# GNN layer with residual and norm on one core: fewer TensorE signals, and GpSimd's gathers no longer tied to the other engines' progress

## The chip, the cores and the metric

One NeuronCore of one Trainium2 chip. Five engines take part: TensorE (PE, with PEld its weight loads), VectorE (DVE), ScalarE (ACT), GpSimd (POOL), and SyncE (SP), which only issues transfers. They run their own streams of instructions and meet by semaphores: an instruction can add one to a semaphore when it is finished (a signal, `then_inc`), another engine waits until the semaphore has reached a value (`wait_ge`). The metric is the device time of one execution in microseconds, the median of several; less is better.

## What is computed

```python
proj = einsum('ni,rio->nro', x, relation_weight)          # x: 50000 x 64, 10 relations
att  = sum(proj[src, etype] * tanh(proj[dst, etype] + efeat), -1)   # 25000 edges
ex   = exp(att - segment_max(att, dst)[dst]);  a = ex / segment_sum(ex, dst)[dst]
h_nb = segment_sum(x[src] * a[:, None], dst)              # dst is sorted
gnn  = leaky_relu((x + h_nb) @ fc.T, 0.01) + leaky_relu((x * h_nb) @ fc2.T, 0.01)
out  = layernorm(x + gnn)
```

A row of x that is nobody's dst has h_nb = 0: its output needs only the dense product with fc. All is float32.

## The kernel before

**Two kinds of work.** The dense part takes the 50,000 rows of x as 49 tiles d of 1024 rows: transpose, product with fc, relu, residual, norm, store. The edge part takes the 25,000 edges as 196 columns of 128 edges, in 25 blocks s of 8 columns (the last has 4). Each dst row that has edges is overwritten at the end with its edge result.

**The steps.** One loop of steps s = -1 to 28 runs on TensorE, ScalarE and VectorE with the same index (PE lines 627 to 701, ACT 814 to 902, DVE 1143 to 1299). In step s stand the relation products of block s, the scores and running sums of block e = s-1, the two residual products of block f = s-2, the norms of l = s-3 and o = s-4, and up to three dense tiles. Dense tiles end in step 15. From LATE = 14 on, the products of a block f take another way (`late_y`, `late_linear`), in the PSUM room that the dense tiles leave. So steps up to 15 are the dense steps, those from 16 the late ones.

**Relation products.** TensorE makes ten "quads" a block (`quad`, L545): four products of 64x64 tiles each, accumulated into t_ps and h_ps. Nine of them read a masked copy of the block's transposed rows, which VectorE makes (`mask`, L989, 9 a block, ring xm of RM = 4 buffers); the fifth (PLAIN_AT = 4) reads an unmasked copy by ScalarE. Mask m may be written once the quad that read mask m-4 has signalled (L995). Quad 9 ends a block: then come ACT's tanh (L710), DVE's product (L1003), PE's scores (L532), the next block's transposes (`turn_in`, L520) and ACT's copy of them (`plain`, L716), and the next block's first mask.

**Signals of TensorE.** Every quad signals (quad_done), as do the edge additions (eadd_done), the transposes (tr_in: three dense tiles and two groups a step, all through one PSUM tile, tr_ps), the dense products (y_done), the scores (att_done), `turn_in` (xT_done) and each quarter of a block's residual products (y12_done). ACT copies out of PSUM what each of them tells of (dT L721, rd L726, uwT L785, l L790), and later PE instructions wait for those copies.

**GpSimd.** POOL issues all indirect transfers, one instruction for a column of 128 rows: 388 gathers of x rows (L450) into a ring xsd of RX = 13 blocks, then 196 scatters of results (L474) from a ring out_r of RW = 18 blocks. Gathering block s waits for the last sum of block s-13 (z2_done, L444). The scatters wait until all dense tiles are stored (L466), and each block's for its result (fmul_done, L470). Besides, POOL is tied to the others' progress: `pace` (L435) makes it wait before an indirect transfer until TensorE has signalled a given place of its stream. The places come from `pe_marks` (L252), which lists all TensorE signals with the count of PE instructions up to each; gather n asks for the mark at n x 14.6 - 250 instructions. `load_e` on SP (L357) waits for eadd_done of three blocks before.

Of the kernel before, what the change touches and what calls it, by code (L numbers as in the profile page):

```python
# [12 lines left out]
P = 128  # L13
# [11 lines left out]
RM = 4  # L25
# [6 lines left out]
PACE, LEAD, PACE_OUT = 14.6, 250, 13.64  # L32
# [8 lines left out]
def gnn_resnorm(nc, x, src, dst, eattr, etype, relw, resw, resw2, out):  # L41
# [17 lines left out]
    def groups(s):  # L59
        return cols(s) // QUAD  # L60
# [4 lines left out]
    Q_BEFORE = [2 * n for n in G_BEFORE]  # L65
# [18 lines left out]
    def quad_count(m):  # L84
        return m // RB * R + m % RB + (2 if m % RB >= PLAIN_AT else 1)

    LATE = (ND - 1) // 3 - 2
    ROW_BLOCKS = [8, 13, 19, 24]
# [20 lines left out]
    with ExitStack() as ctx:  # L109
# [105 lines left out]
        xT_done, masked, quad_done, eadd_done = sem("xT_done"), sem("masked"), sem("quad_done"), sem("eadd_done")  # L215
# [35 lines left out]

        def pe_marks():  # L252

            marks, work, ends = [], [0], {}

            def mark(done, value, instructions):
                work[0] += instructions
                marks.append((done, value, work[0]))

            for s in range(-1, LAST + 1):  # L260
                main, e, f, d = 0 <= s < NS, s - 1, s - 2, tiles(s)
                quarters = 2 * groups(f) if 0 <= f < NS else 0

                def turned(k):
                    if len(d) > k:
                        mark(tr_in, TR_DENSE[d[k]] + 1, 8)

                def multiplied(k):
                    if len(d) > k:
                        mark(y_done, d[k] + 1, 16)  # L270

                def quads(first, last):
                    if main:
                        for r in range(first, last):
                            mark(quad_done, s * R + r + 1, 16)

                def paired(q):
                    if quarters > q:
                        mark(y12_done, Q_BEFORE[f] + q + 1, 8)

                turned(0)
                if main:
                    mark(eadd_done, s + 1, 2 * cols(s))
                if 0 <= e < NS:
                    mark(att_done, e + 1, 2 * cols(e))
                multiplied(0)
                quads(0, 4)
                if quarters > 0:
                    mark(tr_in, TR_PAIR[f, 0] + 1, 8)
                quads(4, 5)  # L290
                if quarters > 2:
                    mark(tr_in, TR_PAIR[f, 1] + 1, 8)
                quads(5, 6)
                paired(0)
                turned(1)
                quads(6, 7)
                paired(1)
                multiplied(1)
                quads(7, 8)
                paired(2)  # L300
                turned(2)
                quads(8, 9)
                paired(3)
                multiplied(2)
                quads(9, 10)
                if 0 <= s + 1 < NS:
                    mark(xT_done, s + 2, 2 * cols(s + 1))
                ends[s] = work[0]
            return marks, ends
# [4 lines left out]
        def _(sp):  # L314
# [42 lines left out]
            def load_e(s):  # L357
                if not 0 <= s < NS:
                    return
                wait(sp, eadd_done, s - RE + 1)  # L360
                c0, n = s * COLS, cols(s)
                n2 = min(n, LASTC - c0)
                done = e_in[s % RE]
                sp.dma_start(ea[0:A0, s % RE, 0:n, :], edge_rows[0:A0, c0:c0 + n, :]).then_inc(done, DMA)
                sp.dma_start(ea[A0:P - 1, s % RE, 0:n, :], edge_rows[A0:P - 1, c0:c0 + n, :]).then_inc(done, DMA)
                if n2 > 0:
                    sp.dma_start(ea[P - 1:P, s % RE, 0:n2, :], edge_last[:, c0:c0 + n2, :]).then_inc(done, DMA)
# [54 lines left out]
        def _(pool):  # L422
# [6 lines left out]
            G_MOVES = [0]  # L429
            for s in range(NS):  # L430
                G_MOVES.append(G_MOVES[-1] + len(columns(s)))

            (marks, ends), at = pe_marks(), [-1]

            def pace(n, scattered_blocks):  # L435
                step_end = ends[min(NS - 1, RW + 4 + scattered_blocks)]
                asked = min(n, G_MOVES[NS]) * PACE + max(n - G_MOVES[NS], 0) * PACE_OUT - LEAD
                need = [k for k, (_, _, work) in enumerate(marks) if work <= min(asked, step_end)]
                if need and need[-1] > at[0]:
                    at[0] = need[-1]  # L440
                    pool.wait_ge(marks[at[0]][0], marks[at[0]][1])

            def gather(s):
                wait(pool, z2_done, s - RX + 1)  # L444
                for k, (j, side) in enumerate(columns(s)):
                    pace(G_MOVES[s] + k, 0)
                    if s == 0 and (j, side) == (0, 1):
                        pool.wait_ge(dst_in, 4 * DMA)
                    c = s * COLS + j
                    pool.indirect_dma_start(  # L450
                        xsd[:, s % RX, j, side, :], None, x[:, :],
                        bass.IndirectOffsetOnAxis(ap=ends_i[:, side, c:c + 1], axis=0),
                    ).then_inc(gathered[s % RX], DMA)
# [15 lines left out]
            def scatter(s):  # L469
                pool.wait_ge(fmul_done, s + 1)  # L470
                for j in range(cols(s)):
                    c = s * COLS + j
                    pace(G_MOVES[NS] + c, s)
                    pool.indirect_dma_start(  # L474
                        out[:, :], bass.IndirectOffsetOnAxis(ap=row_i[:, c:c + 1], axis=0),
                        out_r[:, s % RW, j, :], None, bounds_check=top, oob_is_err=False,
                    ).then_inc(scattered[s % RW], DMA)
# [21 lines left out]
        def _(pe):  # L499
# [36 lines left out]
            def add_edges(s):  # L536
                pe.wait_ge(e_in[s % RE], E_NEED[s])
                wait(pe, tanh_done, s)
                half = cols(s) // 2
                for i in range(half):  # L540
                    mm = pe.matmul(h_ps[:, i * P:(i + 1) * P], ea[:, s % RE, 2 * i:2 * i + 2, :].rearrange("p h f -> p (h f)"),  # L541
                                   ident[:, :], start=(i == 0), stop=False, skip_group_check=True)
                mm.then_inc(eadd_done, 1)

            def quad(s, at):  # L545
# [16 lines left out]
                mm.then_inc(quad_done, 1)  # L562
# [36 lines left out]
            def late_y(f, g):  # L599
# [7 lines left out]
                mm.then_inc(y12_done, 1)  # L607

            def late_linear(f, g):
# [4 lines left out]
                mm.then_inc(y12_done, 1)  # L614
# [89 lines left out]
        def _(act):  # L704

            def tanh(e):
                n = cols(e) // 2 * P
                act.wait_ge(quad_done, (e + 1) * R)
# [3 lines left out]
            def plain(s):  # L712
                n = cols(s) * P
                act.wait_ge(xT_done, s + 1)
                wait(act, quad_done, (s - 1) * R + PLAIN_AT + 1 if s > 0 else 0)
# [189 lines left out]
        def _(v):  # L905
# [83 lines left out]
            def mask(s, r):  # L989
# [5 lines left out]
                wait(v, quad_done, quad_count(m - RM) if m >= RM else 0)  # L995
# [112 lines left out]
            def late_first(f):  # L1108
                n = cols(f)
                v.wait_ge(y12_done, Q_BEFORE[f] + groups(f))  # L1110
# [206 lines left out]
```

## Time and profile before

| what | value |
|---|---|
| median of 3 runs | 890.75 us (890.29 to 2936.04) |
| the profiled execution's span | 908.0 us |
| PE / DVE / ACT / POOL busy in it | 642.8 / 608.1 / 514.2 / 572.8 us |
| granted TensorE clock, mean | 0.844 |
| HBM read and written | 45.60 and 25.78 MB |

The span is that of one profiled execution, from its first to its last instruction, and lies 17.3 us over the median of the runs. Busy time is the union of an engine's instructions; "idle before" is the time an engine stood still just before an instruction, and the arrow names what ended it: another engine's instruction, "issue" (nothing that the profile shows) or "remote" (a semaphore reached its value at that moment, but no instruction that signals it ended just then).

### The profile page before, as it was taken

The numbers are of one execution on the slowest core, as the hardware profiler recorded it, in microseconds if no ns is written. First come the engines' busy times: TensorE is split into PE (matmuls) and PEld (weight loads), VectorE is DVE, ScalarE is ACT, GpSimd is POOL, SyncE is SP. The second block draws the span as 40 slices with busy tenths as digits, with TensorE's granted clock in tenths as the row PEclk, the third lists the DMA queues.
The fourth block names the chain that finished last, engine by engine and source line by source line (L and its number), as shares of the span: only waits on it lengthen the run. The fifth ranks groups of instructions, "written<-read, shape, count | busy, mean of one in ns | idle before, by whom it ended". The sixth has DMA issues, their size and how long they took to land. (4 is left out here: it accounts for less than half of the span.)

```text
span 908.0 us, 13811 instructions
## 1 busy us (share of the span) xinstructions
PE 642.8 (71%) x3948; PEld 356.0 (39%) x3948; DVE 608.1 (67%) x1094; ACT 514.2 (57%) x1457; POOL 572.8 (63%) x594
## 2 busy tenths in 40 slices
PE   2587778877777877877887876877788778865030
PEld 1434343544443443443443443343344344344020
DVE  2459768778778868869778769865686567754050
ACT  0255575577677667767677677744455244555052
POOL 7466666666666666666666666666666666666726
PEclk9788988798998998999897989879987889786555
DMA  5332432333332432432432421321111110000000
GB/s 139 107 101 71 115 103 81 114 103 81 115 103 81 116 104 69 127 103 67 128 104 60 123 81 45 104 73 64 50 48 43 62 57 28 27 29 28 24 6 17
DMA packets 48035, 70.37 MB, mean 77 GB/s; under 512 B 15971, under 2 KB 19487, under 8 KB 47959
## 3 DMA queue, kind: packets, MB, share of 16 engines
q1 hardware_dynamic: 18562, 32.97, 11.6%
q0 software_dynamic: 18752, 17.29, 9.1%
q10 hardware_dynamic: 10644, 19.23, 5.7%
q8 instruction: 32, 0.52, 0.2%
q14 instruction: 45, 0.36, 0.1%
HBM read 45.60 MB, written 25.78 MB: 79 GB/s over the span
## 5 line engine op out<-in xcount | busy, mean ns | idle before, releaser
L450 POOL DMA_INDIRECT xsd<-in_x,ends_i x388 | 378.4, 975 | 219.4 <-issue 91.1
L558 PE MATMUL t_ps<-xm,w_rel 64*64 64x512 f32 (+1 forms) x900 | 263.1, 682 | 17.7 <-DVE xm L996 9.2
L996 DVE SCALAR_TENSOR_TENSOR xm<-typ,xT_ps 128x1024 f32<-128x1024 f32 (+1 forms) x225 | 264.4, 1185 | 14.6 <-ACT xc L716 9.9
L560 PE MATMUL h_ps<-xm,w_rel 64*64 64x512 f32 (+1 forms) x900 | 264.3, 682 | 0.7 <-issue 0.4
L474 POOL DMA_INDIRECT out<-out_r,row_i x196 | 191.3, 976 | 110.4 <-issue 51.7
L575 PE MATMUL y_ps<-bd_cat,dT 128*128 128x256 f32 x392 | 127.0, 481 | 48.1 <-issue 28.6
L575 PEld LDWEIGHTS y_ps<-bd_cat,dT 128*128 128x128 f32 x392 | 89.3, 239 | 69.6 <-issue 33.8
L558 PEld LDWEIGHTS t_ps<-xm,w_rel 64*64 64x64 f32 x900 | 57.8, 149 | 118.4 <-issue 81.9
L740 ACT ACTIVATE o_t<-zd,rstd 128x64 f32<-128x64 f32 x392 | 98.8, 340 | 0.0
L585 PE MATMUL tr_ps<-ident,uw 128*128 128x128 f32 x196 | 35.9, 312 | 70.3 <-DVE uw L1090 31.9
L1058 DVE TENSOR_TENSOR zd<-rd,y_ps 128x512 f32<-128x512 f32 x49 | 33.4, 681 | 57.5 <-issue 29.8
L585 PEld LDWEIGHTS tr_ps<-ident,uw 128*128 128x128 f32 x196 | 23.3, 155 | 112.0 <-issue 75.9
L785 ACT COPY uwT<-tr_ps 128x512 f32<-128x512 f32 x49 | 28.4, 580 | 67.9 <-PE tr_ps L585 33.6
L1003 DVE TENSOR_TENSOR prod<-t_ps,g_t 128x512 f32<-128x512 f32 (+1 forms) x25 | 17.0, 680 | 71.8 <-issue 42.3
L1038 DVE SCALAR_TENSOR_TENSOR es<-es,wd,wx 128x64 f32<-128x64 f32 x196 | 55.4, 282 | 11.7 <-DVE es L1038 0.5
L595 PEld LDWEIGHTS s_ps<-bd_both,uwT 128*128 128x128 f32 x224 | 32.2, 207 | 75.9 <-issue 70.0
L541 PE MATMUL h_ps<-ident,ea 128*128 128x128 f32 x196 | 31.1, 307 | 41.0 <-issue 24.0
L710 ACT ACTIVATE g_t<-h_ps 128x512 f32<-128x512 f32 (+1 forms) x25 | 14.7, 587 | 80.3 <-remote 77.7
L595 PE MATMUL s_ps<-bd_both,uwT 128*128 128x128 f32 x224 | 43.1, 319 | 23.3 <-issue 23.3
L560 PEld LDWEIGHTS h_ps<-xm,w_rel 64*64 64x64 f32 x900 | 58.0, 149 | 3.5 <-issue 3.5
L726 ACT ACTIVATE rd<-y_ps 128x512 f32<-128x512 f32 x49 | 28.9, 590 | 46.4 <-remote 20.2
L764 ACT ACTIVATE wx<-xsd,wd 128x64 f32<-128x64 f32 x196 | 52.1, 338 | 0.8
(161 smaller groups left out, 982.8 us busy)
## 6 DMA issues: line engine op xcount, KB each, us to landing
x_in<-in_x SPq DMA_DIRECT2D x48, 256.0 KB
typ<-typ_d SPq DMA_DIRECT2D x24, 512.0 KB
out<-o_t ACTq DMA_DIRECT2D x48, 256.0 KB
xsd<-in_x SPq DMA_DIRECT2D x512, 0.2 KB
xsd<-in_x,ends_i POOLq DMA_INDIRECT x388
hist<-es ACTq DMA_DIRECT2D x24, 256.0 KB
ea<-in_edge_attr SPq DMA_DIRECT2D x24, 224.0 KB
out<-out_r,row_i POOLq DMA_INDIRECT x196
```

What stands on the lines that cost most here:

```text
L450: pool.indirect_dma_start(xsd[:, s % RX, j, side, :], None, x[:, :], bass.IndirectOffsetOnAxis(ap=ends_i[:, side, c:c + 1], axis=0),).then ...
L474: pool.indirect_dma_start(out[:, :], bass.IndirectOffsetOnAxis(ap=row_i[:, c:c + 1], axis=0), out_r[:, s % RW, j, :], None, bounds_check=t ...
L558: pe.matmul(t_ps[h * D:(h + 1) * D, 0:n], w[0:D, :], moving[0:D, h * n:(h + 1) * n], start=(at == 0), stop=(at == R - 1), skip_group_check ...
L560: mm = pe.matmul(h_ps[(1 - h) * D:(2 - h) * D, 0:n], w[D:P, :], moving[D:P, (1 - h) * n:(2 - h) * n], start=False, stop=(at == R - 1), ski ...
L575: mm = pe.matmul(y_ps[:, j * 2 * P:(j + 1) * 2 * P], dT[:, d % 2, j * P:(j + 1) * P], bd_cat.rearrange("p k f -> p (k f)"), start=True, st ...
L585: mm = pe.transpose(tr_ps[:, j * P:(j + 1) * P], uw[:, g * QUAD + j, :, :].rearrange("p k f -> p (k f)"), ident[:, :])
L595: mm = pe.matmul(s_ps[:, YQ + j * P:YQ + (j + 1) * P], uwT[:, q // 2, k * P:(k + 1) * P], bd_both[:, :], start=True, stop=True)
L740: ins = act.activation(o_t[:, d % RO, j * D:(j + 1) * D], zd[:, d % RZ, j * D:(j + 1) * D], ACT.Copy, scale=rstd[:, s % 2, d % 3, j:j + 1])
L764: ins = act.activation(wx[:, j, :], xsd[:, e % RX, j, 0, :], ACT.Copy, scale=wd[:, e % 2, 0, j:j + 1])
L996: v.scalar_tensor_tensor(xm[:, m % RM, 0:n], typ[:, s % RT, 0:n], float(r), xT_ps[:, 0:n], ALU.is_equal, ALU.mult).then_inc(masked, 1)
L1038: v.scalar_tensor_tensor(es[:, e % RS, j, :], old, wd[:, e % 2, 1, j:j + 1], wx[:, j, :], ALU.mult, ALU.add).then_inc(chain_done, 1)
L1058: v.tensor_tensor(zd[:, d % RZ, :].rearrange("p (j f) -> p j f", j=4), rd[:, d % 2, :].rearrange("p (j f) -> p j f", j=4), y_ps.rearrange( ...
```

## The change

TensorE signals less. Of a block's ten quads only those at places 1, 4, 7 and 9 signal; who waited for another one now waits for the next that signals. `add_edges` no longer signals: SP's `load_e` waits for the first signalling quad of the same block instead. In `late_y` and `late_linear` only the last group of a block signals, and `late_first` and the count Q_BEFORE are fitted to it. The order of work on every engine stays. And `pe_marks` and `pace` are removed: POOL issues its gathers and scatters as soon as the rings, the dense stores and the results allow.

```diff
-PACE, LEAD, PACE_OUT = 14.6, 250, 13.64
...
-    def quad_count(m):
-        return m // RB * R + m % RB + (2 if m % RB >= PLAIN_AT else 1)
+    POSTS = [1, PLAIN_AT, 7, R - 1]
+
+    def quads_until(s, at):
+        return len(POSTS) * s + sum(1 for n in POSTS if n < at) + 1
+
+    def mask_read(m):
+        return quads_until(m // RB, m % RB + (1 if m % RB >= PLAIN_AT else 0))
...
-    Q_BEFORE = [2 * n for n in G_BEFORE]
+    Q_BEFORE = [0]
+    for s in range(NS):
+        Q_BEFORE.append(Q_BEFORE[-1] + (2 * groups(s) if s < LATE else 2))
...
-        def pe_marks():
...
-                wait(sp, eadd_done, s - RE + 1)
+                wait(sp, quad_done, quads_until(s - RE, 0) if s >= RE else 0)
...
-            def pace(n, scattered_blocks):
...
-                    pool.wait_ge(marks[at[0]][0], marks[at[0]][1])
...
-                    pace(G_MOVES[s] + k, 0)
...
-                    pace(G_MOVES[NS] + c, s)
...
-                mm.then_inc(eadd_done, 1)
...
-                mm.then_inc(quad_done, 1)
+                if at in POSTS:
+                    mm.then_inc(quad_done, 1)
...
-                mm.then_inc(y12_done, 1)
+                if g == groups(f) - 1:
+                    mm.then_inc(y12_done, 1)
...
-                act.wait_ge(quad_done, (e + 1) * R)
+                act.wait_ge(quad_done, quads_until(e, R - 1))
...
-                wait(v, quad_done, quad_count(m - RM) if m >= RM else 0)
+                wait(v, quad_done, mask_read(m - RM) if m >= RM else 0)
...
-                v.wait_ge(y12_done, Q_BEFORE[f] + groups(f))
+                v.wait_ge(y12_done, Q_BEFORE[f] + 1)
```

## Rows read from the trace of the kernel before

**Rows 1.** The page, part 1: busy time, share of the span and instructions.
```profile
PE 642.8 (71%) x3948; PEld 356.0 (39%) x3948; DVE 608.1 (67%) x1094; ACT 514.2 (57%) x1457; POOL 572.8 (63%) x594
```

**Rows 2.** Waits of all engines: who waited for whom, us, times, longest.
```profile
POOL xsd L450 <- remote: 69.4, 48, 4.1
```

**Rows 3.** Timeline, first masks of blocks 0, 1, 2, 3, 15, 16, 24: start, us.
```profile
42.67 4.62 DVE L996 SCALAR_TENSOR_TENSOR xm<-typ,xT_ps 128x1024 f32<-128x1024 f32 x4
...
72.06 2.34 DVE L996 SCALAR_TENSOR_TENSOR xm<-typ,xT_ps 128x1024 f32<-128x1024 f32 x2
...
135.98 2.34 DVE L996 SCALAR_TENSOR_TENSOR xm<-typ,xT_ps 128x1024 f32<-128x1024 f32 x2
...
550.09 2.34 DVE L996 SCALAR_TENSOR_TENSOR xm<-typ,xT_ps 128x1024 f32<-128x1024 f32 x2
...
577.30 2.35 DVE L996 SCALAR_TENSOR_TENSOR xm<-typ,xT_ps 128x1024 f32<-128x1024 f32 x2 [1.13 <-ACT xc L716]
...
801.45 1.28 DVE L996 SCALAR_TENSOR_TENSOR xm<-typ,xT_ps 128x512 f32<-128x512 f32 x2
```

**Rows 4.** Busy time by stretch (us, PE, PEld, DVE, ACT, POOL, clock) in a dense step.
```profile
345.00:380.00 35.00, 28.23 (x175) 15.62 (x178) 27.59 (x49) 25.97 (x78) 21.95 (x23) 0.90 0.31 90
```

**Rows 5.** Timeline of step 10's end: TensorE's signals and who takes them.
```profile
396.98 0.59 PE L558 MATMUL t_ps<-xm,w_rel 64*64 64x512 f32 x1
397.52 0.71 PE L595 MATMUL s_ps<-bd_both,uwT 128*128 128x128 f32 x4
398.07 0.60 PE L568 MATMUL tr_ps<-ident,x_in 128*128 128x128 f32 x4
...
400.55 0.37 ACT L790 COPY l<-s_ps 128x256 f32<-128x256 f32 x1 [2.02 <-remote]
402.03 0.59 ACT L721 COPY dT<-tr_ps 128x512 f32<-128x512 f32 x1 [1.10 <-remote]
402.26 0.94 POOL L450 DMA_INDIRECT xsd<-in_x,ends_i  x1 [1.52 <-remote]
```

**Rows 6.** Timeline of the start, where POOL gathers without a pause.
```profile
20.52 3.74 PE L575 MATMUL y_ps<-bd_cat,dT 128*128 128x256 f32 x8 [2.02 <-ACT dT L721]
24.09 0.60 PE L568 MATMUL tr_ps<-ident,x_in 128*128 128x128 f32 x4
...
27.89 0.95 POOL L450 DMA_INDIRECT xsd<-in_x,ends_i  x1 [0.31 <-issue]
```

**Rows 7.** Timeline of the start, ScalarE.
```profile
26.73 0.60 ACT L726 ACTIVATE rd<-y_ps 128x512 f32<-128x512 f32 x1 [6.26 <-remote]
32.66 0.59 ACT L721 COPY dT<-tr_ps 128x512 f32<-128x512 f32 x1 [5.33 <-remote]
```

**Rows 8.** Timeline of the tail, where POOL scatters without a pause.
```profile
832.33 3.62 PE L606 MATMUL y_ps<-bd_relu,uwT 128*128 128x128 f32 x16
...
837.20 1.00 PE L613 MATMUL tr_ps<-bd_lin,uwT 128*128 128x64 f32 x8
...
844.05 0.69 DVE L1111 SCALAR_TENSOR_TENSOR zf<-y_ps,xsd 128x512 f32<-128x512 f32 x1 [6.16 <-remote]
...
861.40 0.97 POOL L474 DMA_INDIRECT out<-out_r,row_i  x1 [0.31 <-issue]
866.60 0.69 DVE L1122 TENSOR_TENSOR zf<-zf,tr_ps 128x512 f32<-128x512 f32 x1 [21.13 <-remote]
```

**Rows 9.** Timeline of step 10: mask 8, and what VectorE does after it.
```profile
395.44 1.21 DVE L996 SCALAR_TENSOR_TENSOR xm<-typ,xT_ps 128x1024 f32<-128x1024 f32 x1
...
398.57 0.69 DVE L1058 TENSOR_TENSOR zd<-rd,y_ps 128x512 f32<-128x512 f32 x1 [1.92 <-issue]
...
404.81 1.23 DVE L1096 SCALAR_TENSOR_TENSOR l<-l 128x1024 f32<-128x1024 f32 x1 [3.13 <-issue]
```

**Rows 10.** The two lines of POOL: duration ns min/median/max, first and last start.
```profile
L450 POOL DMA_INDIRECT xsd<-in_x,ends_i x388: 942/947/1533, 3.5 to 599.3; - x194
...
L474 POOL DMA_INDIRECT out<-out_r,row_i x196: 971/974/1185, 600.5 to 902.3; - x196
```

More of the change, by code:

```diff
@@ L214, in gnn_resnorm @@
         scattered = sems("scattered", RW)
-        xT_done, masked, quad_done, eadd_done = sem("xT_done"), sem("masked"), sem("quad_done"), sem("eadd_done")
+        xT_done, masked, quad_done = sem("xT_done"), sem("masked"), sem("quad_done")
         tanh_done, prod_done, att_done, max_done = sem("tanh_done"), sem("prod_done"), sem("att_done"), sem("max_done")
@@ L250, in o_need @@
             return sum(len(x_parts(d)) for d in mine) * DMA
-        def pe_marks():
[L254 to L309, printed above, removed]
         block = ctx.enter_context(nc.Block())
@@ L427, in _ @@
                                channel_multiplier=1).then_inc(before_done, 1)
[L429 to L433, printed above, removed]
-            def pace(n, scattered_blocks):
[L436 to L440, printed above, removed]
-                    pool.wait_ge(marks[at[0]][0], marks[at[0]][1])
             def gather(s):
                 wait(pool, z2_done, s - RX + 1)
-                for k, (j, side) in enumerate(columns(s)):
-                    pace(G_MOVES[s] + k, 0)
+                for j, side in columns(s):
                     if s == 0 and (j, side) == (0, 1):
@@ L540, in add_edges @@
                 for i in range(half):
-                    mm = pe.matmul(h_ps[:, i * P:(i + 1) * P], ea[:, s % RE, 2 * i:2 * i + 2, :].rearrange("p h f -> p (h f)"),
+                    pe.matmul(h_ps[:, i * P:(i + 1) * P], ea[:, s % RE, 2 * i:2 * i + 2, :].rearrange("p h f -> p (h f)"),
                                    ident[:, :], start=(i == 0), stop=False, skip_group_check=True)
-                mm.then_inc(eadd_done, 1)
             def quad(s, at):
@@ L613, in late_linear @@
                     mm = pe.matmul(tr_ps[:, j * D:(j + 1) * D], uwT[:, g, k * P:(k + 1) * P], bd_lin[:, :], start=True, stop=True)
-                mm.then_inc(y12_done, 1)
+                if g == groups(f) - 1:
+                    mm.then_inc(y12_done, 1)
             def pair_part(f, q):
@@ L714, in plain @@
                 act.wait_ge(xT_done, s + 1)
-                wait(act, quad_done, (s - 1) * R + PLAIN_AT + 1 if s > 0 else 0)
+                wait(act, quad_done, quads_until(s - 1, PLAIN_AT) if s > 0 else 0)
                 act.copy(xc[:, 0:n], xT_ps[:, 0:n]).then_inc(plain_done, 1)
```

## The prediction

> **What bounds the kernel now.** I read the page first, then the waits, the first masks of the blocks, one dense step, and the start and the tail instruction by instruction. No engine is busy more than 71% of the span: PE 642.8 us, DVE 608.1, POOL 572.8 [rows 1]. So it isn't an engine's work but the order between engines that sets the time. A dense step takes 34.5 us: (550.09 - 135.98)/12; a late one 28.0: (801.45 - 577.30)/8 [rows 3]. In 35 us of dense steps PE is busy 28.2 and DVE 27.6 [rows 4], so 6 to 7 us of each dense step are waiting.
>
> What is waited for? The reader should take one signal of TensorE and look when its reader starts. In step 10 PE's L595 ends at 397.52 + 0.71 = 398.23, and the ACT copy of it, which had stood idle for 2.02 us, starts at 400.55: 2.3 us late. The transposes of L568 end at 398.67, their copy starts at 402.03: 3.4 us late [rows 5]. "remote" says the same: the semaphore moved while nothing that signals it ended. The second moved only as POOL stood still; it goes on at 402.26, after 1.52 us of idle [rows 5].
>
> The start and the tail show it without other work. POOL gathers without a pause up to 28.84 [rows 6]. PE's L575 ends at 24.26, its ACT reader starts at 26.73, 2.5 us late; L568 ends at 24.69, its reader starts at 32.66, 8.0 us late, though idle for 5.33 [rows 6, 7]. In the tail POOL scatters without a pause up to 862.37. The second L606 group ends at 835.95, VectorE's L1111 starts at 844.05; the last L613 ends at 838.20, L1122, idle for 21.13, starts at 866.60 [rows 8]. Between them lie four signals of PE in a row (L606, L613, L677, L613): (866.60 - 835.95)/4 = 7.7 us each. So I read: **TensorE's signals are held up while POOL issues indirect transfers, pass one at a time, and get through when POOL pauses.** Its pauses today are the waits of `pace` (69.4 us behind "remote" alone [rows 2]), so that tie also lets signals through.
>
> **The change, part by part.**
> *Fewer signals.* A dense step has 25 now: 10 quads, eadd, xT, att, 5 tr_in, 3 y, 4 y12. Six quads and eadd go: 18. A late one has 10 + eadd + xT + att + 2 tr_in + 4 y12 = 19, after it 4 + 1 + 1 + 2 + 2 = 10.
> *Later waits for the masks.* Mask 8 now waits for quad 7 instead of quad 5. In step 10 it starts at 395.44; quad 7 ends at 396.98 + 0.59 = 397.57, and its signal comes up to 2.3 later: 2.1 to 4.4 us later on DVE [rows 5, 9]. Behind it on DVE wait dense_add L1058, its sums and L1096. Two idle stretches take it up, 1.92 and 3.13 us [rows 9], so I charge 1 us a dense step (0 if all is taken up, 4.4 if none: 66 us over 15 steps). The other waits that move up (masks 4, 5, 6, 7 of a block, 0 and 2 of the next) find their quads over. `load_e` now waits for quad 1 of three blocks before, two steps old: nothing, and nothing for the typ and x loads queued behind it on SP. The late products are read as whole blocks, except late_first, which needs just the last L606 group: nothing.
> *POOL untied.* It saves POOL its pauses, worth nothing in itself: 584 indirect transfers at 1.25 to 1.28 us from start to start (0.95 or 0.97 and 0.30 or 0.31 of issue [rows 6, 8, 10]) are 740 us, well inside the span. What it costs is the pauses for the signals. POOL now runs in three stretches.
>
> *Stretch 1, gathers without a pause.* A block's 16 gathers take 20 us, block g starts at 5 + 20g, and only from block 13 on does it wait, for the end of step g-11. One signal in this regime costs between 0.1 us (nothing at all) and 7.7 [rows 8]; I take 2.3, which the running step shows [rows 5] and the start nearly repeats (2.5 [rows 6, 7]). A step's 18 signals one behind the other are then 18 x 2.3 = 42 us, over the 34.5 of now. The first mask is at 43 [rows 3], say 45. POOL is caught by the ring when (t-5)/20 - 10 = (t-45)/42: t = 350, with 7.3 steps done.
> *Stretch 2, gathers gated by the ring.* A step holds 20 us of gathers, in which 20/42 of it gets done, and the rest runs with POOL silent. A step without POOL I take as 30 us: the first lasted 29.4 (72.06 - 42.67 [rows 3]), PE's own work is 28.2 [rows 4], plus the 1 us of mask 8. So 20 + (1 - 20/42) x 30 = 35.7 us a step. The gate for block 24 opens at the end of step 13: 350 + 6.7 x 35.7 = 589. Step 14, beside the last gathers: 625. Step 15 without POOL: 655. Block 16 starts there instead of at 577.3 [rows 3]: **+78 us.**
> *Stretch 3, scatters.* They start when the dense tiles are stored, in step 16, and twelve blocks are ready at once. But 10 signals x 2.3 = 23 us are less than a late step's 28.0, so signals no longer set it; I take off 1 us for each of 9 steps (0 to 3): **-9.**
> *Tail.* At 10.2 us a block, POOL has caught up by step 23. So there are pauses in the tail, and 3 signals instead of 5 around the 28.4 us between 838.20 and 866.60 [rows 8]. Between 0 and 22 us of these go; I take **-12.** The last 21 transfers stay.
> Sum: 908.0 + 78 - 9 - 12 = 965 us of span; the runs' median lies 17.3 below it: **948 us.**
>
> For the price of a signal there is a rule in the Trainium skill, "TensorE: Matmul & The Clock Gate", The cost: per-tile semaphore tail: increments of one semaphore after another come about 26 ns apart. By that estimate a step's 18 signals would be 0.5 us, the 195 removed ones 5 us in all, and untied POOL would cost nothing. "SBUF - State Buffer", Who interferes with whom, says that PE never waits on anyone; that is about memory ports. Neither speaks of a signal that is held up, and the trace has 2.3 to 8.0 us where they would have 0.03.
>
> **Rivals.**
> 1. *The signals become cheap enough: faster.* If their removal counts for more than the lost pauses, a step in stretch 1 falls below 34.5. For it: 7 of 25 signals go, and the first steps took 29.4. Against it: at the start, nearly empty of signals, one was 8 us late. At 33 us a step: caught at 451 with 12.3 done, steps of 31.8, block 16 at 567: -10, with -9 and -12: 877 of span, 860 us. A price of a few hundredths of a microsecond, the skill's rule, leads here too.
> 2. *Even.* At 36 us a step, 2.0 us a signal: caught at 405, 10 done, steps of 33.3, block 16 at 602: +24 - 21, so 894 us. That is the point that decides: dearer than 2.0 us and it is slower.
> 3. *Mask 8 sets the step.* If DVE's idle doesn't take up its wait, up to 3.4 us more in 15 steps: 948 + 51 = 999 us. For it: DVE is as full as PE [rows 4]. Against it: 5 us of idle right behind it.
> 4. *Signals at 7.7 us, the tail's price.* Steps of 139 us until POOL has filled the ring at 265, then 30 until the gate opens, then 20 + (1 - 20/139) x 30 = 45.7: block 16 at 885 (+308), the first twelve scattered blocks +78, seven late steps +39: 1316 us. For it: two long stretches show it; against it: there PE was idle, and the running step shows 2.3.
>
> **How the numbers follow.** The forecast, 948, has 0.42; rival 3 0.10, rival 4 0.13, even 0.15, faster 0.20. So faster 0.20, within 2% 0.15, slower 0.65 (2%, some 18 us, is about what a measurement of this kernel tells from no change). The range: at 3.4 us a signal, the larger number of rows 5, a step is 61 us: caught at 283 with 3.9 done, steps of 40.2, block 16 at 759, +182 - 21, 1052 us. Down it takes in most of the faster case: 855. So 855 to 1055. The likeliest's own range is 915 to 1055.
>
> **What would show it.** Right: POOL's gathers 1.25 us apart without a pause to some 350 us, then sixteen and a pause a step; steps over 34.5 us in the first stretch and under 36 in the second; ACT's and DVE's idle "remote" grown; block 16's first mask near 655; no 21 us hole before L1122. Mask 8 right behind quad 7. Wrong: steps near 30 us while POOL runs without a pause (signals aren't held up by it, or not one at a time), or first steps over 60. The sum hangs most on the price of a signal, 0.3 us of which are 30 to 55 us at the end.

## The result, and the profile after

The changed kernel takes 1276.06 us (1273.49 to 1278.28 in four runs) against 890.79 us before: 1.433 times the time (95% interval 1.428 to 1.438), 385 us slower. The profiled execution has a span of 1276.6 us; before it was 908.0. One of before's four runs took 2936 us and is left out of the ratio; nothing in this study explains it.

The page after: busy time, and four lines of its 40 slices of 31.9 us (tenths busy; PEclk is the granted clock). It answers to [rows 1].

```profile
PE 716.3 (56%) x3948; PEld 360.6 (28%) x3948; DVE 605.4 (47%) x1094; ACT 512.1 (40%) x1457; POOL 566.7 (44%) x594
...
PE   2120431206857967778778776887300278888740
...
DVE  2001001005876755686557755897110066677642
...
POOL 7777777720043234422443234202777604222456
PEclk9555655558988777987778777999555579888855
```

DVE, ACT and POOL do the work of before in the time of before (608.1, 514.2 and 572.8 us then). PE takes 73.5 us longer for its 3948 matmuls, at a mean granted clock of 0.735 against 0.844. What grew most is the time in which nothing runs. Where POOL shows 7 or 6 from slice 1 to 8 and from 29 to 32, the other engines show little or nothing, and from slice 2 on the granted clock there is 5 or 6 tenths, which is at or near the lower of its two levels (1.2 of 2.4 GHz).

The longest waits after: engine and line, who ended them, us, times, longest. Before, `xm` waited 4.4 us behind "remote" in all, and POOL's 69.4 us [rows 2] were the tie. Masks are now L930, gathers L383, scatters L406.

```profile
DVE xm L930 <- remote: 403.8, 20, 94.4
POOL xsd L383 <- DVE zf L1040: 327.2, 12, 92.8
...
ACT uwT L719 <- remote: 156.0, 12, 30.0
POOL out L406 <- ACT out_r L744: 140.2, 10, 34.2
```

20 waits of VectorE hold 404 us, more than the whole loss of 385: they end when a signal is seen that TensorE gave long before.

First masks of blocks 0, 1, 3, 14, 16, 18 and 24 after, from the timeline (start, us); compare [rows 3].

```profile
115.95 1.22 DVE L930 SCALAR_TENSOR_TENSOR xm<-typ,xT_ps 128x1024 f32<-128x1024 f32 x1 [21.55 <-issue]
...
309.57 1.21 DVE L930 SCALAR_TENSOR_TENSOR xm<-typ,xT_ps 128x1024 f32<-128x1024 f32 x1
...
361.63 1.21 DVE L930 SCALAR_TENSOR_TENSOR xm<-typ,xT_ps 128x1024 f32<-128x1024 f32 x1
...
811.06 1.21 DVE L930 SCALAR_TENSOR_TENSOR xm<-typ,xT_ps 128x1024 f32<-128x1024 f32 x1
...
864.01 1.21 DVE L930 SCALAR_TENSOR_TENSOR xm<-typ,xT_ps 128x1024 f32<-128x1024 f32 x1
...
1040.78 1.22 DVE L930 SCALAR_TENSOR_TENSOR xm<-typ,xT_ps 128x1024 f32<-128x1024 f32 x1 [0.76 <-ACT xc L650]
...
1196.12 0.68 DVE L930 SCALAR_TENSOR_TENSOR xm<-typ,xT_ps 128x512 f32<-128x512 f32 x1
```

The same blocks began at 42.67, 72.06, 135.98, 514.80, 577.30, 630.31 and 801.45 before. The 368.6 us of span divide like this:

| Stretch | before | after | difference | POOL meanwhile |
|---|---|---|---|---|
| start to block 0 | 42.7 | 115.9 | +73.3 | gathers without a pause |
| block 0 to 1 | 29.4 | 193.6 | +164.2 | the same, 117 of them |
| 1 to 3 | 63.9 | 52.1 | -11.9 | almost silent: steps of 24.3 and 27.7 |
| 3 to 14 | 378.8 | 449.4 | +70.6 | 16 gathers a step |
| 14 to 16 | 62.5 | 53.0 | -9.5 | silent: 28.6 and 24.4 |
| 16 to 18 | 53.0 | 176.8 | +123.8 | 104 scatters without a pause |
| 18 to 24 | 171.1 | 155.3 | -15.8 | 8 scatters a step |
| 24 to the end | 106.5 | 80.5 | -26.1 | 44 scatters left instead of 64 |

The two runs without a pause, at the start and from 882 to 1015 us, cost 361 us. The eleven steps from block 3 to 14, with 16 gathers in a row each, add 70.6, and the other four stretches give 63.3 back. Where POOL is silent a step is faster than before; the granted clock there is 1.00, where before's dense step has 0.90 [rows 4].

The start after, ScalarE and TensorE and at the end VectorE's mask 4 of block 0, shows how little passes; compare [rows 6, 7].

```profile
37.01 3.78 PE L507 MATMUL y_ps<-bd_cat,dT 128*128 128x256 f32 x8 [11.81 <-issue]
...
58.76 0.60 ACT L660 ACTIVATE rd<-y_ps 128x512 f32<-128x512 f32 x1 [21.27 <-remote]
...
69.96 0.59 ACT L655 COPY dT<-tr_ps 128x512 f32<-128x512 f32 x1 [10.60 <-remote]
...
70.59 3.78 PE L507 MATMUL y_ps<-bd_cat,dT 128*128 128x256 f32 x8 [28.96 <-issue]
...
92.36 0.60 ACT L660 ACTIVATE rd<-y_ps 128x512 f32<-128x512 f32 x1 [21.29 <-remote]
...
125.96 0.59 ACT L655 COPY dT<-tr_ps 128x512 f32<-128x512 f32 x1 [10.05 <-remote]
...
170.76 0.60 ACT L660 ACTIVATE rd<-y_ps 128x512 f32<-128x512 f32 x1 [44.21 <-remote]
...
215.56 1.22 DVE L930 SCALAR_TENSOR_TENSOR xm<-typ,xT_ps 128x1024 f32<-128x1024 f32 x1 [94.40 <-remote]
```

L507 ends at 40.79 and its reader, idle, starts 18.0 us later; the next time at 74.37, and 18.0 later again. In the other direction nothing is late: ScalarE's copy ends at 69.96 + 0.59 = 70.55, and TensorE starts on it at 70.59.

The trace also has the moment at which a semaphore moved. In this run of 207 gathers without a pause, from 3.5 to 266.6 us, TensorE's signals do pass, one at a time and in the order in which they were given: the recorded ones are seen at 58.73, 69.93, 92.33, 114.73, 125.94, 170.73 and 215.53, so 11.2, 22.4 or 44.8 us apart. The last of these is quad 1's, given at 132.75, on which mask 4 waits. The end of the run does not free the rest at once: the next two, given at 195.55 and 228.51, are seen at 281.33 and 293.97, 15 and 27 us after POOL's last gather. Why the intervals are multiples of 11.2 us no run tells.

A step of the second stretch, whose burst of 16 gathers runs from 399.11 to 418.88:

```profile
399.11 0.94 POOL L383 DMA_INDIRECT xsd<-in_x,ends_i  x1 [21.11 <-DVE zf L1040]
...
413.33 1.01 PE L489 MATMUL t_ps<-xc,w_rel 64*64 64x512 f32 x1 [1.72 <-issue]
...
414.75 1.01 PE L489 MATMUL t_ps<-xc,w_rel 64*64 64x512 f32 x1 [0.40 <-issue]
...
417.94 0.94 POOL L383 DMA_INDIRECT xsd<-in_x,ends_i  x1 [0.30 <-issue]
...
421.79 1.22 DVE L930 SCALAR_TENSOR_TENSOR xm<-typ,xT_ps 128x1024 f32<-128x1024 f32 x1 [13.76 <-remote]
421.98 0.59 ACT L719 COPY uwT<-tr_ps 128x512 f32<-128x512 f32 x1 [13.29 <-remote]
```

ScalarE and VectorE both stand idle for over 13 us and go on 0.2 us apart, 3 us after the burst's last transfer. The trace's semaphore updates tell which signals they wait for: TensorE gave one at 404.74 and the next at 411.62, and they show at 421.77 and 421.96.

### The profile page after: what moved, and what is told of

It is laid out like the page before. It is cut to its first block and busy times, and to the rows that moved or that the text cites. A ratio compares the mean times of both kernels' runs of the same rounds, so it can differ in the third digit from the quotient of the medians.

```text
span 1276.6 us, 13782 instructions
## 1 busy us (share of the span) xinstructions
PE 716.3 (56%) x3948; PEld 360.6 (28%) x3948; DVE 605.4 (47%) x1094; ACT 512.1 (40%) x1457; POOL 566.7 (44%) x594
## 5 line engine op out<-in xcount | busy, mean ns | idle before, releaser
L383 POOL DMA_INDIRECT xsd<-in_x,ends_i x388 | 372.2, 959 | 442.9 <-DVE zf L1040 327.2
L930 DVE SCALAR_TENSOR_TENSOR xm<-typ,xT_ps 128x1024 f32<-128x1024 f32 (+1 forms) x225 | 264.4, 1185 | 497.4 <-remote 403.8
L489 PE MATMUL t_ps<-xm,w_rel 64*64 64x512 f32 (+1 forms) x900 | 273.9, 673 | 85.3 <-issue 55.1
L406 POOL DMA_INDIRECT out<-out_r,row_i x196 | 191.4, 977 | 261.7 <-ACT out_r L744 140.2
L491 PE MATMUL h_ps<-xm,w_rel 64*64 64x512 f32 (+1 forms) x900 | 275.4, 675 | 25.8 <-issue 25.8
L507 PE MATMUL y_ps<-bd_cat,dT 128*128 128x256 f32 x392 | 103.7, 411 | 148.9 <-issue 90.3
L507 PEld LDWEIGHTS y_ps<-bd_cat,dT 128*128 128x128 f32 x392 | 76.0, 204 | 165.5 <-issue 103.3
L491 PE MATMUL h_ps<-xc,w_rel 64*64 64x512 f32 (+1 forms) x100 | 55.4, 736 | 31.6 <-issue 31.3
L489 PE MATMUL t_ps<-xc,w_rel 64*64 64x512 f32 (+1 forms) x100 | 53.2, 718 | 32.5 <-issue 32.0
L655 ACT COPY dT<-tr_ps 128x512 f32<-128x512 f32 x49 | 28.9, 589 | 106.2 <-remote 95.4
L660 ACT ACTIVATE rd<-y_ps 128x512 f32<-128x512 f32 x49 | 28.6, 584 | 97.4 <-remote 88.3
L491 PEld LDWEIGHTS h_ps<-xm,w_rel 64*64 64x64 f32 x900 | 51.8, 144 | 37.5 <-issue 37.5
L698 ACT ACTIVATE wx<-xsd,wd 128x64 f32<-128x64 f32 x196 | 52.1, 338 | 0.8
L744 ACT ACTIVATE out_r<-zcf,rstd 128x64 f32<-128x64 f32 x196 | 49.1, 333 | 0.0
```

Source lines behind the costliest of these rows:

```text
L383: pool.indirect_dma_start(xsd[:, s % RX, j, side, :], None, x[:, :], bass.IndirectOffsetOnAxis(ap=ends_i[:, side, c:c + 1], axis=0),).then ...
L406: pool.indirect_dma_start(out[:, :], bass.IndirectOffsetOnAxis(ap=row_i[:, c:c + 1], axis=0), out_r[:, s % RW, j, :], None, bounds_check=t ...
L489: pe.matmul(t_ps[h * D:(h + 1) * D, 0:n], w[0:D, :], moving[0:D, h * n:(h + 1) * n], start=(at == 0), stop=(at == R - 1), skip_group_check ...
L491: mm = pe.matmul(h_ps[(1 - h) * D:(2 - h) * D, 0:n], w[D:P, :], moving[D:P, (1 - h) * n:(2 - h) * n], start=False, stop=(at == R - 1), ski ...
L507: mm = pe.matmul(y_ps[:, j * 2 * P:(j + 1) * 2 * P], dT[:, d % 2, j * P:(j + 1) * P], bd_cat.rearrange("p k f -> p (k f)"), start=True, st ...
L698: ins = act.activation(wx[:, j, :], xsd[:, e % RX, j, 0, :], ACT.Copy, scale=wd[:, e % 2, 0, j:j + 1])
```

## The experiments

The runs were made on five chips of two kinds, which the kernel before tells apart: some 890 us on two (5 and 1), as in the result, and 909 us in its single execution on chip 7; 764 and 765 us on two others (6 and 3). On the second kind all 371 recorded signals of TensorE in the changed kernel's trace are visible within 0.15 us, with POOL running without a pause. Below, the first are called chips that hold, the others chips that don't.

The theory after the result: while POOL issues indirect transfers back to back, TensorE's signals don't pass at a price each; after a few transfers nothing passes until POOL pauses. The tie gave the pauses. Taken word for word the rows above already refute it, since in the run of 207 gathers a signal does pass every 11 to 45 us; what the experiments can show is whether short runs with pauses bring the signals back. Rivals: the fewer signals or the later waits for masks cost the time; it is a price per signal, only larger; it is any work of POOL.

### One part alone, and pauses by filler, on a chip that doesn't hold

`e1_signals` is after's signals with before's tie, `e2_untied` before's signals without the tie. For `e2_untied`:

```diff
-                    pace(G_MOVES[s] + k, 0)
...
-                    pace(G_MOVES[NS] + c, s)
```

and for `e1_signals` the changed kernel gets both calls back, with `pe_marks` naming only the signals that are left:

```diff
+                            if r in POSTS:
+                                mark(quad_done, quads_until(s, r), 16)
+                            else:
+                                work[0] += 16
```

The other two are the changed kernel with POOL kept busy by fills of an unused tile:

```diff
+            issued = [0]
+
+            def rest():
+                issued[0] += 1
+                if issued[0] % 4 == 0:
+                    for n in range(4):
+                        wait(pool, rest_done, (issued[0] // 4 - 1) * 4 + n)
+                        pool.memset(rest_t[:, :], 0.0).then_inc(rest_done, 1)
```

called after every gather and scatter. This is `e3_rest4`: four fills of 128x400 after every fourth transfer, each of which waits for the fill before it. `e4_rest1` has one fill of 128x160 after each transfer.

> The fewer signals and the later waits that follow from them, with POOL still tied to the others' progress by the numbers of before (its marks are those signals that are left). Theory A (a TensorE signal passes at once while POOL rests or has just begun to issue, and is held once POOL has issued some four or five indirect transfers without a pause, until POOL pauses): the tie keeps the runs of transfers short, so the time stays near that of before, 865 to 895 us, a little less for 195 signals that can't be held. Theory B (it is mask 8's wait for quad 7, and the other later waits, that cost): slower, 950 us or more, since they are all here. Theory C (each signal that is left costs its own price, 7 us and more): with 18 instead of 25 signals a step clearly faster, under 860 us.

> All signals of before, only POOL's tie taken out. Theory A: POOL again issues 208 gathers without a pause, then sixteen a step, then 100 scatters, and nothing of TensorE gets through in them but every 10 to 50 us: about as slow as the changed kernel, 1200 to 1400 us, and slower than it where the held signals are more (a step before its first mask needs the same ones, a quad now has one each). Theory B: near before, about 890 us. Theory C: 25/18 of the lost time, so 1400 us or more.

> The changed kernel, and after each fourth indirect transfer POOL fills a small scratch tile four times (about 2 us in all), tied to nobody's progress. Theory A: four transfers and a rest are 7 us, in which every signal gets through, at the latest in the rest; 584 transfers are then 584/4 x 7 = 1020 us of POOL, which becomes the bound: 1030 to 1070 us, with steps of about 30 us while POOL runs. If POOL's being busy at all holds the signals, not its indirect transfers, there is no relief: 1276 + 146 x 2 us x the part of it on the path, over 1350. Theory B: as the changed kernel or worse, 1276 and more.

> The changed kernel, and after each indirect transfer one short fill of a scratch tile (about 0.25 us), tied to nobody's progress: 584 x 1.5 = 880 us of POOL. If a held signal needs only a gap of any length between two transfers: 900 to 950 us. If, as in the trace of before, it needs a stretch of more than a microsecond without a transfer: as bad as the changed kernel, 1276 us and up to 120 us more.

Measured, against 764.16 us: 762.96 (ratio 0.9987, 0.9975 to 1.0000), 764.36 (1.0005, 0.9988 to 1.0022), 1022.21 (1.338, 1.334 to 1.342) and 830.35 (1.087, 1.083 to 1.090). Neither part does anything here: what was expected of them missed, since this chip holds no signals. What stays of these runs: from block 5 on, dense steps of 28.1 to 28.6 us in both `e1_signals` and `e2_untied`, so the mask's later wait costs nothing on this chip; and with the fills POOL itself is the bound (830.6 us busy in `e3_rest4`, 726.8 in `e4_rest1`, and its waits on top).

### The same parts on a chip that holds

> The changed kernel itself once more, beside the kernel before. In the last comparison the kernel before took 764 us instead of 891, and no TensorE signal came late in any trace: that was another chip. If this one is like that, theory A' (the hold-up of signals belongs to the chip, not to the kernel) expects 755 to 775 us for all of before, after and untied with all signals, and mask 8's wait for quad 7 to cost nothing to 10 us. If this one is like the first: before near 891, this 1276.

> All signals of before, no tie. On a chip that holds signals up, theory A: 1200 to 1400 us, like the changed kernel (the loss comes with the missing tie). If it came with the fewer signals or mask 8's later wait: near 891. On a chip that does not: 764.

> Signals of after, tie of before. On a chip that holds signals up, theory A: 865 to 895 us; theory B (the later waits cost): 950 and more. On a chip that does not: 763.

> The changed kernel with a rest of POOL after each fourth indirect transfer, tied to nobody. POOL's own time bounds it at about 1022 us, as measured on the chip without hold-up. On a chip that holds signals up, theory A: the same 1022 to 1060 us, far below 1276, since each signal gets through within a rest; if a rest by other POOL work does not let them through: over 1400.

One profiled execution each, beside 909.31 us of the kernel before: 1277.85, 1262.34, 906.18 and 1017.75 us. So the lost tie alone is the loss, and the fewer signals alone are worth nothing; single executions are enough to tell 350 us from none, not to tell 3 us. `a2_untied` lies within its expectation, `a3_signals` above 865 to 895, as before itself does here, and `a4_rest4` 4 us below its range. The waits of `a2_untied`, first lines, are those of after:

```profile
POOL xsd L375 <- DVE zf L1030: 325.3, 12, 92.7
DVE xm L920 <- remote: 295.9, 27, 72.0
ACT uwT L709 <- remote: 210.1, 12, 81.8
```

`a4_rest4` gives POOL no tie, only a pause of 2.07 us after every fourth transfer. Its page, TensorE and VectorE in slices of 25.4 us:

```profile
PE   2877888888787888878798988738510000000000
...
DVE  2877998899898989988888888746610000000010
```

The steps are back: block 24 starts at 702.05, where before had 801.45 [rows 3] and after 1196.12. TensorE's steps are over in slice 30, at some 745 us, and the rest is POOL catching up, as it was in `e3_rest4`. The same code gives 1018 here and 1022 on the other chip, so with such pauses the holding no longer sets the time.

### How long a pause, how often (chip 5, before 892.72 us)

> The changed kernel, with one short fill of a scratch tile by POOL (0.25 us) after each indirect transfer; the same kernel took 830 us on the chip that holds nothing up, where POOL's own time bounds it. On a chip that holds signals up (before near 891): if any gap between two transfers lets a held signal through, 830 to 870 us, faster than both kernels. If it takes a longer stretch without a transfer, 1276 to 1400 us.

> The changed kernel, one fill of 0.5 us after each fourth transfer: POOL's own time is 745 + 146 x 0.5 and its start, about 820 us. With hold-up: if it takes a stretch of over 1 us from the end of a transfer, as the trace of before suggests (its pauses last 1.3 to 1.7 us, and the signals come at their end), no relief: 1200 to 1350 us. If a shorter one is enough: 830 to 900 us.

> The same with two fills, 0.95 us, after each fourth transfer: POOL's own time 890 us. With hold-up: signals come through in most of the rests, steps of 30 to 34 us, POOL is the bound: 885 to 930 us. If the rest has to be longer: over 1000 us.

> The same share of rest as the one before, but 1.9 us after each eighth transfer: POOL's own time 890 us again. Theory A (signals pass up to the fourth transfer of a run, none later): each run of 10 us has 5 us in which nothing gets through, so steps of 36 to 42 us and 950 to 1100 us with hold-up, against 885 to 930 for the rests after four. If only the share of rest counts, the two are the same.

In a name such as `rest8x4` the first number says after how many transfers POOL fills, the second how many fills of 128x400 it makes; `rest1` has one of 128x160.

| Kernel | median gap between transfers with a fill | us | ratio (95%) |
|---|---|---|---|
| c1_rest1 | 0.41 us after each | 1211.17 | 1.356 (1.341 to 1.371) |
| c2_rest4x1 | 0.61 us after every 4th | 1251.13 | 1.401 (1.389 to 1.413) |
| c3_rest4x2 | 1.09 us after every 4th | 931.37 | 1.043 (1.030 to 1.055) |
| c4_rest8x4 | 2.07 us after every 8th | 954.41 | 1.069 (1.058 to 1.079) |

Without a filler the gap is 0.30 us. It is not the sum of the pauses that counts: 0.41 after each is 1.6 us in four transfers, more than the 1.09 of `c3_rest4x2`, and brings 65 us of the 385 where the latter brings 345 (against the 1276 us of the result; the changed kernel itself was not run on chip 5). A gap of 1.09 us in one piece after every fourth transfer is enough for most of the loss and one of 0.61 is not; between the two nothing was tried. Nor is it a fixed price per signal: the signals are the same in all four. `c2_rest4x1` and `c4_rest8x4` came out as expected, `c3_rest4x2` 1 us above its range, and `c1_rest1` below the 1276 us expected of no relief, so short gaps help a little.

POOL's own rows in `c2_rest4x1` hold a second finding:

```profile
124.35 0.94 POOL L393 DMA_INDIRECT xsd<-in_x,ends_i  x1 [0.30 <-issue]
126.45 0.43 POOL L385 MEMSET rest_t<- 128x400 f32 x1 [1.16 <-remote]
127.12 0.95 POOL L393 DMA_INDIRECT xsd<-in_x,ends_i  x1 [0.24 <-issue]
```

The fill waits for the signal of the fill before it, four transfers back, and this came late: 6.0 us after its end. Of some 100 recorded signals of POOL in this trace 34 were late, of TensorE's 366 it is 85, of ScalarE's 459 and VectorE's 771 none. So POOL's own signals are held too, and in this trace those of the two other engines aren't. Here the pauses of 1.6 to 2.3 us which that wait made at 125 to 153 us brought no mask either: quad 1's signal, given at 113.65, let mask 4 start only at 181.03. A pause long enough behind four transfers elsewhere is not enough here, and why isn't settled.

### Another form of transfer, and the tail

`d1_after` is the changed kernel on a chip that doesn't hold. In `d2_plain` POOL gathers with plain transfers of successive rows (so the edges get other rows than theirs):

```diff
-                    pool.indirect_dma_start(
-                        xsd[:, s % RX, j, side, :], None, x[:, :],
-                        bass.IndirectOffsetOnAxis(ap=ends_i[:, side, c:c + 1], axis=0),
-                    ).then_inc(gathered[s % RX], DMA)
+                    pool.dma_start(xsd[:, s % RX, j, side, :], x[c * P:(c + 1) * P, :]).then_inc(gathered[s % RX], DMA)
```

`d3_tail` is `e1_signals` with three fills after every fourth of the scatters 151 to 171, to let the tail's signals through:

```diff
+                    if 150 <= c <= 172 and c % 4 == 3:
+                        rest()
```

> The changed kernel once more. Where the kernel before takes some 764 us (a chip that holds no signal up), theory A' expects 755 to 775 us: neither the missing tie nor mask 8's later wait costs there anything. Where it takes 891: 1276 again.

> The changed kernel, with each of POOL's 388 indirect gathers replaced by a plain transfer of 128 successive rows of x into the same place, also issued by POOL (so the edges get other rows than they should). It tells whether it is the indirect form that holds signals. If any transfer issued by POOL does it: 1200 to 1350 us where before takes 891, with a first stretch as slow as the changed kernel's. If only the indirect form does: the first stretch runs with steps of about 28 us, the scatters alone hold signals, and the time is 850 to 1000 us.

> The fewer signals with the tie of before, and POOL rests 1.4 us after every fourth of the scatters 151 to 171, in the tail, where the tie asks for nothing any more. With hold-up: the hole of VectorE before late_third of block 22 (21 us in the trace of before) shrinks to under 8 us, because the signals it waits for pass in a rest; POOL then bounds the tail, so the gain is small: 0 to 10 us (ratio 0.99 to 1.0). If the hole stays, it was not the hold-up. Without hold-up: 8 us slower at most, since POOL's last run gets six rests.

Against 765.04 us: `d1_after` 764.63 (0.9992, 0.9982 to 1.0003), `d2_plain` 750.99 (0.982, 0.980 to 0.984), `d3_tail` 771.69 (1.0091, 1.0074 to 1.0108). The whole change is worth nothing on such a chip; the plain transfers gain 14 us; the fills cost 6.7 against the kernel before. The same three questions on chip 1, which holds (before 889.99 us): `f1_plain` is `d2_plain`, `f2_tail` is `d3_tail`, and `f3_signals` is `e1_signals`.

> As the run before with the plain gathers, for a chip that holds signals up (before near 891). Any transfer issued by POOL holds them: 1200 to 1350 us. Only the indirect form: steps of about 28 us up to the scatters, 850 to 1000 us. Without hold-up 751 us, as measured.

> As the run before with the rests in the tail, for a chip that holds signals up: VectorE's 21 us hole in the tail under 8 us, ratio to before 0.985 to 1.0. Without hold-up 1.009, as measured.

> The fewer signals with the tie of before, timed for a ratio on a chip that holds signals up: one look gave 906.2 us beside 909.3 of before, so 0.99 to 1.0. If 7 of 25 signals a step less were worth something where each can be held: 0.98 or less. Without hold-up 0.999, as measured.

`f1_plain` took 886.43 us in its one run. Its two lines of POOL's transfers (busy us, mean ns, idle before and what ended it):

```profile
L383 POOL DMA_DIRECT2D xsd<-in_x x388 | 209.0, 548 | 209.7 <-DVE zf L1037 208.5 <-DMA ends_i<-in_src 1.1
L403 POOL DMA_INDIRECT out<-out_r,row_i x196 | 191.9, 979 | 265.4 <-ACT out_r L741 139.6 <-DMA out<-o_t 69.4 <-issue 56.4
```

Its page, slices of 22.1 us:

```profile
PE   2888898888878987898888630003397887787430
...
DVE  2788999999999999999999401000377676776530
...
POOL 8999953331233213331000677777122233333465
```

POOL shows 9 in slices 2 to 5, with 85 transfers back to back from 16.66 to 62.41, and TensorE 8 there: no signal waits, the dense steps take 23.2 to 28.6 us, and block 16 starts at 471.9 (577.30 before). Then come the scatters, still indirect, in one run from 490.48 on, and TensorE shows 3000: the step from block 17 to 18 takes 155 us, as after's. In one execution the plain form leaves the signals alone and the indirect one holds them. What in the indirect form does it, no run tells.

`f2_tail` took 894.72 us (1.0076, 1.0044 to 1.0108), `f3_signals` 896.09 (1.0054, 1.0006 to 1.0101); both ratios were expected at or below 1.0. They differ from each other by the fills alone, and by 1.4 us, which is inside their scatter. In the trace of `f3_signals` the tail's hole is there, 21.86 us before the row that was L1122. In that of `f2_tail` it is gone, as expected:

```profile
829.97 0.69 DVE L1144 SCALAR_TENSOR_TENSOR zf<-y_ps,zf 128x512 f32<-128x512 f32 x1
830.69 0.69 DVE L1150 TENSOR_TENSOR zf<-zf,tr_ps 128x512 f32<-128x512 f32 x1
```

That row started at 866.60 before [rows 8]. Still the run is hardly shorter. POOL has its last scatters to issue one behind the other, and now 18 fills besides; that this is the reason is argued, not shown.

## Why the prediction was wrong

It said slower, 948 us, and it was slower by nearly seven times as much; 1276 lies far outside 855 to 1055. Point by point:

**The mechanism was right.** That `pace` gave TensorE's signals their pauses is what `a2_untied` and `a4_rest4` show. The half sentence "pass one at a time" holds as well: the seven signals seen in after's first run come one by one.

**The step that failed is the price of a signal in stretch 1: 2.3 us, "which the running step shows".** In its place stand 11.2 to 44.8 us from one signal seen to the next, and up to 86 us from the end of a quad to its reader. The 2.3 was measured in runs of mostly four to six transfers with a pause of 1.3 to 1.7 us behind them, and used in a run of 207. By the semaphore updates, a signal given when no other was waiting, during before's first transfer of a run, is seen at once in 42 of 60 cases, at the second in 26 of 64, the third 14 of 47, the fourth 10 of 38, the fifth in none of 10; after's trace has 15 of 15 at the first, and from the fifth on 2 of some 25. The mean of some 1.8 us before is mostly the rest of a short run. The price depends on the length of the run, and the change was about just that length. So steps of 42 us until 350, with 7.3 done, became a first mask at 115.95 and one step of 193.6 us with the ring full at 267: +237.5 us by block 1. Block 16 began 286.7 us later than before, where +78 was forecast.

**Rival 4 had the mechanism's size.** It priced a signal at 7.7 us, from the only two long runs of before [rows 6 to 8], and gave steps of 139 us, the ring full at 265, block 16 at 885 and 1316 us. Measured: 194, 267, 864 and 1276. That the total lies so near is in part luck: the rival had the first mask at 45 instead of 115.95 and the first scattered blocks at +78 instead of +123.8, and against that the late steps at +39 instead of -15.8 and nothing for the tail instead of -26.1. Its 7.7 is also an average over two regimes. Of the four signals behind it two were seen in the run of scatters, at 844.03 and 858.05, so 8.1 and 14.0 us after the one before; the other two at 862.97 and 866.51, when the run had ended at 862.37. Still, the rows that pointed the right way were on the table, with 8.0 and 7.7 us, and were given 0.13 since "there PE was idle". The forecast went by where the kernel spent its time before; it should have gone by the regime into which the change moves it.

**Stretch 2** was 35.7 us a step and is 41.0: (811.06 - 401.26)/10, 401.26 being block 4. Half of it failed with the price: in 20 us of gathers about 7 us of a silent step of 28 get done, not 20/42 of it. The other half was too dear: the 30 us of a silent step are 24.3 and 27.7 after, so 41.0 is 20 of burst and 21 of the rest.

**Stretch 3** was -9, since 10 signals x 2.3 are less than a step. It is +108 (123.8 - 15.8): the ready blocks make one run of 104 scatters, and the step beside them lasts 155 us. The later steps do gain, 25.9 us each against 28.5, with 8 scatters in a step.

**Fewer signals, mask 8.** `a3_signals` (906.18 beside 909.31), `f3_signals` (1.0054) and `e1_signals` (0.9987) say that 195 signals less bring nothing. That pauses every few transfers let every waiting signal through, however many there are, would explain it and is not shown. And mask 8, charged at 1 us a step, costs nothing in `e1_signals`, whose dense steps are those of `e2_untied`; on a chip that holds this was not separated.

For the price of one signal there is the rule of the Trainium skill, "TensorE: Matmul & The Clock Gate", The cost: per-tile semaphore tail, of some 26 ns an increment, which makes 195 signals 5 us at most, by estimate. A chip that doesn't hold is in keeping with that bound: `e1_signals` measures -1.2 us, 0 to -1.9. On a chip that holds, 18.0 us for one signal at the start are some 700 times the rule's figure.

**Tail.** -12 us was for the 21 us hole. After, 26 us go, and there are 20 scatters fewer left (20 x 1.28 = 25.6 us of POOL, which ends the run); the hole shrank to 4.8 us. But `f2_tail` takes the hole out of before's order, and its timed runs are not faster than before's. One reading fits: before's profiled execution lies 17.3 us above its timed runs, about the 15.6 us that POOL stands idle behind the hole, while `f2_tail`'s profiled one (893.77) lies at its median. The hole may then exist in profiled executions only. No run shows it.

**The marks.** The text said "wrong: first steps over 60", and they were. Of the marks for right, the gathers without a pause (to 267 us, not 350) and then sixteen and a pause came, the grown "remote", the tail without a 21 us hole, and mask 8 less than 0.2 us behind quad 7 in most blocks up to 17; block 16 near 655 and steps under 36 didn't.

Open: why some chips hold and others don't; what in an indirect transfer does it; why the early pauses of `c2_rest4x1` brought nothing; and what share of the long steps is TensorE's own slow pace, told in the last section. A version that is better on both kinds wasn't found. Untied with a pause of about 1 us every fourth transfer (931 us) comes nearest on a chip that holds, and before's tie beats it (893 on the same chip), at no cost on a chip that doesn't hold: 764.16 us with it, 764.36 without (`e2_untied`).

## What to carry to other kernels

A wait that throttles one engine can be what lets another engine's signals through: before such a tie is taken out, look in the trace for readers that start late behind "remote" and ask what the throttled engine was doing. A delay measured in a regime holds for that regime: price a change by the rows nearest to the regime that it leads into, even if they are few and at the edge of the trace. And time a kernel on more than one chip: here one kernel gave 764 or 890 us, and one change 0% or 43%.

## What was not expected of the hardware

Two kinds of chips: 764 against 890 us for the same kernel. On the first, no signal of TensorE was late in the changed kernel's trace (371 of 371 recorded), with 584 indirect transfers back to back; on the second 71 of 358, and in before's 377 of 503.

The signals held for long are those of two engines, TensorE's and POOL's own. Of ScalarE's and VectorE's recorded ones none was over 0.3 us late in before, after and `c2_rest4x1`; `a3_signals` and `f2_tail` have one of ScalarE's each at 1.0 to 1.2 us. But their records thin out on these chips: of VectorE's 1028 signals 570 have one in before's trace, 1016 in that of `d1_after`.

TensorE itself runs slowly in a long run of POOL. In after's first long step the three quads behind quad 1, 24 matmuls with their masks ready by 120.6, end at 195.55, 62.8 us after quad 1. Matmuls of `c2_rest4x1`, with nothing that the profile shows to wait for:

```profile
115.92 0.59 PE L503 MATMUL h_ps<-xm,w_rel 64*64 64x512 f32 x1 [1.42 <-issue]
118.72 1.01 PE L503 MATMUL h_ps<-xm,w_rel 64*64 64x512 f32 x1 [2.21 <-issue]
121.52 1.01 PE L501 MATMUL t_ps<-xm,w_rel 64*64 64x512 f32 x1 [1.79 <-issue]
```

They start 2.80 us apart, where at 110.5 four start within 0.02 us; after's at 413.33 and 414.75 are 1.42 apart. Whether the held signals slow the engine or one cause does both, no run tells. The long waits of the readers still end with held signals: in that step of after, mask 4 waits for a signal that is 82.8 us old when it is seen, and mask 6 for one of 85.8 us.

Signals pass while POOL runs two or more fills in a row (`c3_rest4x2`, `a4_rest4`); a plain transfer of POOL takes 0.548 us against 0.959 for an indirect one after, and holds nothing either.
